# A fused attention and mixture-of-experts kernel: third group's operands stacked ahead of two weight quarters, twelve early scores, early first expert weights

## The reference, cut to what matters

```python
x = x + cross_attention(layernorm(x), ctx, ctx, k_length)     # x, ctx: (8, 256, 512)
x = x + moe(layernorm(x), gate_w, w1, b1, w2, b2, wd, wu, sw1, sb1, sw2, sb2, swd, swu)

# cross_attention: 8 heads of 32 rows per batch; out = softmax(s * q^T k) v, s = SCALE * log(k_length)
# moe, over T = 2048 tokens of D = 512:
probs = softmax(xt @ gate_w); top_p, top_i = top_k(probs, 2)       # 8 experts
for k in range(2):                                                 # capacity 320 per choice and expert
    h = gelu(buf @ w1 + b1); y = h @ w2 + b2 + gelu(buf @ wd) @ wu
    out += y[slot of the token] * keep * top_p[:, k]
sh = gelu(xt @ sw1 + sb1) @ sw2 + sb2 + gelu(xt @ swd) @ swu       # shared expert, for all tokens
out += 0.2 * sh
```

## Time and profile before

| | |
|---|---|
| median of 3 runs | 1408.8 us (1408.75 to 1411.6) |
| the profiled execution | 1401.34 us, span 1399.5 us |
| PE busy | 1346.4 us, 96% of the span |
| DVE busy | 812.6 us, 58% |
| ACT busy | 687.5 us, 49% |
| POOL busy | 249.1 us, 18% |
| mean granted clock of PE | 0.992 |

### The profile page before, as it was taken

The page is one execution under the profiler, slowest core; times in us unless marked ns, Lnnn a source line. Parts: engine busy times, 40 slices in busy tenths (PEclk is TensorE's granted clock), DMA queues, the critical chain, the costliest instruction groups (busy, mean ns, idle before and its releaser), DMA issues.

```text
span 1399.5 us, 27035 instructions
## 1 busy us (share of the span) xinstructions
PE 1346.4 (96%) x11193; PEld 967.1 (69%) x11211; DVE 812.6 (58%) x1313; ACT 687.5 (49%) x1023; POOL 249.1 (18%) x219
## 2 busy tenths in 40 slices
PE   5788999999999999999999999999999999999997
PEld 2152737364645555384788889998888888888895
DVE  7776778686978777762743625536255362452620
ACT  5866666667575756561523524335243342432511
POOL 4720010000000000452201304013030030300202
PEclk9999999999999999999999999999999999999999
DMA  9613131413131222118735665466454565553402
GB/s 273 203 37 100 52 93 39 113 39 106 46 96 49 84 54 92 24 25 213 233 102 124 168 131 157 126 149 164 130 157 109 134 178 131 151 132 99 99 6 38
DMA packets 136731, 155.89 MB, mean 111 GB/s; under 512 B 59049, under 2 KB 79673, under 8 KB 136610
## 3 DMA queue, kind: packets, MB, share of 16 engines
q1 hardware_dynamic: 124322, 128.97, 31.7%
q0 software_dynamic: 12288, 25.21, 9.6%
HBM read 109.47 MB, written 34.15 MB: 103 GB/s over the span
## 4 chain that ended last, share of the span: by engine, by line
PE 81%; DVE 8%; ACT 5%; issue 2%; DMA 1%; SPq 1%; POOL 1%; POOLq 0%; ACTq 0%; DVEq 0%
PE banks L1722 25%; PE banks L1752 24%; PE banks L1641 9%; PE banks L1659 6%; PE banks L1581 4%; PE banks L1561 3%; PE banks L1529 3%; DVE rowmax L1192 2%; DVE late_stage L1213 2%; ACT hidden L982 2%; PE banks L1774 1%; ACT QS L969 1%; PE banks L1615 1%; PE banks L1590 1%; SPq L801 1%
## 5 line engine op out<-in xcount | busy, mean ns | idle before, releaser
L1752 PE MATMUL banks<-hidden,w2h 128*128 128x0 bf16 x2048 | 313.0, 273 | 0.0
L982 ACT ACTIVATE hidden<-banks,scales 128x512 f32<-128x512 f32 x256 | 170.1, 686 | 111.8 <-PE banks L1561 92.4
L1752 PEld LDWEIGHTS banks<-hidden,w2h 128*128 128x128 bf16 x2048 | 198.4, 98 | 25.7
L1752 PE MATMUL banks<-hidden,w2l 128*128 128x0 bf16 x1024 | 195.7, 273 | 0.0
L1192 DVE TENSOR_REDUCE rowmax<-banks 128x1 f32<-128x512 f32 x256 | 172.7, 684 | 37.3 <-PE banks L1529 35.4
L1343 DVE TENSOR_TENSOR w1l<-stage,w1h 128x2048 bf16<-128x2048 f32 x32 | 73.4, 2292 | 199.7 <-ACT w1h L1058 199.7
L1075 ACT ACTIVATE hf<-banks,b1cols 128x640 f32<-128x640 f32 x128 | 101.7, 794 | 178.0 <-PE banks L1722 172.3
L1659 PE MATMUL banks<-w2h,hidden 128*128 128x512 bf16 x512 | 185.4, 381 | 0.0
L1082 ACT ACTIVATE yT<-banks 128x640 f32<-128x640 f32 (+1 forms) x32 | 22.1, 691 | 270.1 <-PE banks L1752 270.1
L1722 PE MATMUL banks<-eth,w1h 128*128 128x0 bf16 x1024 | 136.2, 276 | 3.2 <-ACT lowf L1065 3.2
L1722 PE MATMUL banks<-etl,w1h 128*128 128x0 bf16 x1024 | 136.8, 277 | 0.0
(11 more groups left out here) (194 smaller groups left out, 1963.3 us busy)
## 6 DMA issues: line engine op xcount, KB each, us to landing
stage<-in_L_ffn_w SPq DMA_DIRECT2D x64, 1024.0 KB, 5.5
split_parts<-hidden SPq DMA_DIRECT2D x16, 512.0 KB, 2.9
QS<-split_parts SPq DMA_DIRECT2D x48, 128.0 KB, 3.1
KS<-split_parts SPq DMA_DIRECT2D x48, 128.0 KB, 3.4
xin<-in_x SPq DMA_DIRECT2D x16, 256.0 KB, 3.6
cin<-in_ctx SPq DMA_DIRECT2D x16, 256.0 KB, 3.1
out_rows<-xin SPq DMA_DIRECT2D x16, 256.0 KB, 2.0
normed_rows<-x2r SPq DMA_DIRECT2D x16, 256.0 KB, 2.8
```

What stands on the lines that cost most here:

```text
L982: ac.activation(prob[n % NPH], bank(score_bank[unit]), ACT.Exp, scale=scales[:, g // 2:g // 2 + 1]).then_inc(s_exp, 1)
L1752: issued = mm(half_of(bank(b0 + j)).shape_from_register(bank_cols(e, j)), w[:, fb, rows], half_of(a[:, fb, :], j).shape_from_register(slot ...
```

## The change

- Quarters 6 and 7 are loaded in the first window, after the third group's `bounce` instead of before it. Quarters 2 to 6 are split in the exponentials' loops, and quarter 7 behind the first `up` block. The waits for the places that quarters 4 to 7 overwrite are counted per quarter.
- `EARLY_FIRST = 12` scores of the third group, instead of 8, run beside the second group's exponentials, from the third exponential on; the up pass of the first window has four fewer.
- `parts` and `rows` of the second group come in the last three units of the first group's loop; `b2_parts` comes at the first exponential of the second group instead of the tenth.
- `route` makes 14 (part 0) and 6 (part 1) empty steps ahead of `place`, instead of one each.
- The first three eighths of expert 0 are loaded at the seventh unit of the last window's up pass, into parts of `hidden` and into `late_stage`. `turn_x` of expert 0 waits until two of them are split. Splits 0 to 2 stand among the last downs, split 3 behind `e_rank` and `wu`.

```diff
+EARLY_FIRST = 12
...
-        yield
+
+        for _ in range(6 if part else 14):
+            yield
         add("place", part)
...
-                    score = scores((g + 1) * UNITS, (g + 1) * UNITS + EARLY)
+                    score = scores((g + 1) * UNITS, (g + 1) * UNITS + (EARLY if w else EARLY_FIRST))
...
-                if i >= (UNITS - EARLY if k else 2 if w else 1):
+                if i >= (UNITS - EARLY if k and w else 2 if k or w else 1):
                     next(score, None)
                     if k == 0 and w == 0 and i < 5:
                         next(score, None)
-                if k == 0 and w:
-                    if i == LATE + 2:
+                if k == 0:
+                    if i == (LATE + 2 if w else UNITS - 3):
                         add("parts", g + 1)
-                    elif i > LATE + 3:
+                    elif i > (LATE + 3 if w else UNITS - 3):
                         next(rows, None)
...
+                    if k == 0 and i == 7:
+
+                        add("w_load", 6)
+                        add("w_load", 7)
                     if k == 0 and i == 13:
                         add("wd", E)
-                    if k == 1 and i == 9:
+                    if k == 1 and i == 0:
                         add("b2_parts")
...
-            for _ in scores((a + 2) * UNITS + EARLY, (a + 3) * UNITS):
+            for _ in scores((a + 2) * UNITS + (EARLY if w else EARLY_FIRST), (a + 3) * UNITS):
...
+            if not more and n == 6:
+                add("first_stages")
...
             if w == 0:
+                if n == 1:
+                    split_quarter(7)
...
-    QUARTERS = (4, 8, 13, 18, 23, 28)
+    QUARTERS = (4, 8, 13, 18, 25)
...
-    for k in range(4, 8):
+    for k in range(4, 6):
         add("w_load", k)
...
     def first_weights():
         add("wd", 0)
-        for q in range(4):
+        for c in range(CH):
+            add("turn_x", 0, c)
+        for q in range(NST):
             for _ in range(6):
                 yield
             add("e_split", q)
-            if q == 0:
-                for c in range(CH):
-                    add("turn_x", 0, c)
...
         add("wu", e)
+        if e == 0:
+            add("e_split", NST)
...
+        first_stages = [hidden[:, 2 * FB * PASS + 2 * NPH * L:][:, 0:4096].bitcast(F32), late_stage[:, :],
+                        hidden[:, 2 * FB * PASS + NPH * L:][:, 0:4096].bitcast(F32)]
...
+                    if e == 0 and c == 0:
+
+                        sp.wait_ge(s_whi, split_no(1))
+                        sp.wait_ge(s_wlo, 2)
...
+                    n = j + NST - 1
+                    if j and n < 8 * E:
+                        sp.wait_ge(s_whi, split_no(n - NST))
+                        sp.wait_ge(s_wlo, n - NST + 1)
+                        load_quarter(n)
+                elif kind == "first_stages":
+
+                    sp.wait_ge(s_ones, len(SUMMED))
+                    sp.wait_ge(s_pv, GROUPS * QT)
+                    for n in range(NST):
+                        load_quarter(n)
...
+                    if n >= 4:
+
+                        pool.wait_ge(s_wlog, 12 if n < 6 else 16)
...
-                    if n == 4:
-                        act.wait_ge(s_wlog, 16)
+                    if n in (4, 6):
+
+                        act.wait_ge(s_wlog, 4 if n == 4 else 8)
```

More of the change, by code:

```diff
@@ L235, in exponentials_and_down @@
                     add("ones", g - 1)
-            if k == 0 and w == 0:
-                add("parts", 1)
             for _ in rows if k == 0 else ():
@@ L628, in build @@
                 w = g // 2
-                first = w == 0 or (unit[0] == "score" and g == 2 and i < EARLY)
+                first = w == 0 or (unit[0] == "score" and g == 2 and i < EARLY_FIRST)
                 if unit[0] == "score" and i < EARLY and g % 2 == 0 and g > 2:
@@ L682, in low_no, with stage_of @@
             return PASSES + e + 1
+        def stage_of(j):
+            return first_stages[j] if j < NST else stage[j % NST][:, :]
         def split_no(j):
@@ L690, in sync_program, with load_quarter @@
             dma = nc.sync.dma_start
+            def load_quarter(n):
+                e, q = divmod(n, 8)
+                src = (w1[e].rearrange("(k p) f -> p k f", p=P)[:, :, q * 512:q * 512 + 512] if q < 4
+                       else w2[e].rearrange("(k p) d -> p k d", p=P)[:, (q - 4) * 4:(q - 4) * 4 + 4, :])
+                dma(stage_of(n).rearrange("p (a w) -> p a w", w=512), src).then_inc(s_stage[n % NST], 16)
             for unit in plan:
@@ L803, in sync_program @@
                     j = unit[1]
-                    for n in range(3) if j == 0 else range(j + 2, j + 3):
-                        if n >= 64:
-                            continue
-                        if n >= NST:
-                            sp.wait_ge(s_whi, split_no(n - NST))
-                            sp.wait_ge(s_wlo, n - NST + 1)
-                        e, q = divmod(n, 8)
-                        src = (w1[e].rearrange("(k p) f -> p k f", p=P)[:, :, q * 512:q * 512 + 512] if q < 4
-                               else w2[e].rearrange("(k p) d -> p k d", p=P)[:, (q - 4) * 4:(q - 4) * 4 + 4, :])
-                        dma(stage[n % NST][:, :].rearrange("p (a w) -> p a w", w=512), src).then_inc(s_stage[n % NST], 16)
+                    n = j + NST - 1
[8 more added lines that the diff above has]
+                        load_quarter(n)
             n = GROUPS + (E - 1) * CH
@@ L1057, in act_program @@
                         dst = w2h[:, (q - 4) * 4:(q - 4) * 4 + 4, :]
-                    ac.activation(dst, stage[j % NST][:, :].rearrange("p (a w) -> p a w", w=512), ACT.Copy).then_inc(s_whi, 1)
+                    ac.activation(dst, stage_of(j).rearrange("p (a w) -> p a w", w=512), ACT.Copy).then_inc(s_whi, 1)
                 elif kind == "e_rank":
@@ L1342, in dve_program @@
                               else (w2l[:, (q - 4) * 4:(q - 4) * 4 + 4, :], w2h[:, (q - 4) * 4:(q - 4) * 4 + 4, :]))
-                    dv.tensor_tensor(lo, stage[j % NST][:, :].rearrange("p (a w) -> p a w", w=512), hi, ALU.subtract).then_inc(s_wlo, 1)
+                    dv.tensor_tensor(lo, stage_of(j).rearrange("p (a w) -> p a w", w=512), hi, ALU.subtract).then_inc(s_wlo, 1)
                 elif kind in ("route", "slot"):
@@ L1459, in shared_bank @@
                     pe.wait_ge(s_exp, 2 * UNITS)
-                    pe.wait_ge(s_max, 2 * UNITS + EARLY)
+                    pe.wait_ge(s_max, 2 * UNITS + EARLY_FIRST)
                 else:
```

## The result

The changed kernel took **1421.89 us** (median of 4 runs, 1420.91 to 1423.84), the kernel before 1408.78 (4 runs, three of them those of the table above; 1408.46 to 1411.6): by the comparison of the runs 1.0081 times as long, 95% interval 1.0059 to 1.0103, which is 8 to 15 us. By the medians it is 13.1 us slower, where 13 us less were forecast. The profiled execution took 1423.84 us, span 1422.0.

What follows compares the result with a forecast made beforehand. PE, busy for nearly the whole span, was taken to bound the kernel. Savings of 7.5 (opening with up pass) + 2.0 (first `place`) + 1.4 (second) + 2.1 (hand-over) = 13.0 us, off the 1408.8 median, gave 1395.8 us, range 1390 to 1403.

Steps and rivals of the forecast that it cites:

- The opening: First window up to and including its up pass: 6.5 us net before the pass plus 1.0 in it, bounds 2 and 11.3.
- Both signs that I had named for being wrong: PE waits for row maxima growing above 5 us in all; first up pass not shorter.
- Removed: 1.6 + 1.9 + 2.75 + 2.9 = 9.2 us: Opening: ACT's wait for POOL, quarter 7's copy, PE's row-maximum wait and the half clock all go; 2.7 us added back.
- The half clock, its largest term: Opening, 70 to 80 us: 5.8 us at the half clock disappear, saving 2.9 us of lost work.
- 1.5 us back for four maxima fewer: First up pass: of 2.1 us that PE waits for row maxima outside the long wait, 1.5 are saved.
- 0.5 us off for quarter 7's low pieces: First up pass: 4.50 us of POOL work moved there slows DVE, costing 0.5 us; net of the pass 1.0.
- First `place`: PE's 2.94 us wait and 1.8 us of clock go, 2.7 us return behind DVE's sum: 2.0 us, bounds 0.2 and 4.7.
- the stalls come back: Rival: waits before the eleventh exponential and third `e_up` each bring 1.8 us of half clock: 1398.9 us, chance 0.15.
- 3 × 1.3 us later: First `place`: POOL's scatters start that much later, covered by the gap before the second part's entries, at no cost.
- Second `place`: Placing two `up` blocks later finds DVE's counts ready, so PE's wait goes: 1.4 us saved.
- Hand-over: Into expert 0: 4.9 us go, 0.3 and 1.9 (third `e_up`) return; 2.1 us taken, bounds −1 and 4.9.
- the landing of the second load: Hand-over: loads for splits 3 and 4, issued near 658.4, land at 663.7 and 666.4; PE then waits 1.9 us.

Runs made afterwards that it cites:

- fourth set: On a slower chip (kernel before 1413.91 us), changed kernel with two loads ahead of the transposes, plus: quarter 7's split moved back, 1415.09; `parts` and `rows` back, 1414.23; both, 1416.26.
- faster kind: The two chips on which the unchanged kernel before took 1400.2 and 1399.8 us; the changed kernel took 1404.42 us on one of them.
- slower kind: The two chips on which the unchanged kernel before took 1412.7, 1413.9 and 1413.9 us in three sets.
- first set: On a slower chip (kernel before 1412.73 us): changed kernel again, 1422.55; with early loads moved back, 1427.13; with both delays undone, 1416.06; kernel before plus hand-over alone, 1412.99.
- the spaced variant: Changed kernel with scatters from the sixth group on held to one per two up blocks, the rest in a burst later: 1411.35 us, 1.0072 times the kernel before.

## Why the prediction was wrong

**The opening (forecast 7.5, measured a loss).** Its parts came much as written: the stacking copies of the third group at 43.23, `b2_parts` in one block (from 53.29, not near 50), no half clock in 70 to 80 us. That the 3.58 us of issuing mean a full ring is a reading that no run tests. But the first `rank` came at 76.44, 1.5 us earlier and not 7, and the up pass took 24.8 us from its first to its last block instead of 22.1. Both signs that I had named for being wrong are there, 5.3 us of waits for row maxima and a pass that isn't shorter. The step that failed is the sum "Removed: 1.6 + 1.9 + 2.75 + 2.9 = 9.2 us": it adds up stalls of engines that wait for one another as if each lay on the path. The idle times in it went, and others took their place. The half clock, its largest term, moved and did not shrink:

```profile
50.00:60.00 10.00, 8.15 (x37) 1.58 (x29) 6.19 (x9) 6.92 (x10) 3.63 (x4) 0.70 0.71 233
90.00:100.00 10.00, 6.95 (x87) 5.47 (x83) 8.31 (x20) 5.72 (x15) 1.58 (x2) 0.83 0.08 28
```

Before, these two stretches had 0.83 and 1.00; over 44 to 104 us the mean granted clock is 0.91 in both kernels, and TensorE is busy 46.7 us before and 46.6 after. At the start, TensorE's timeline after:

```profile
48.60 0.41 PE L1576 MATMUL banks<-identb,MS 128*32 128x128 bf16 x16 [1.91 <-DVE MS L1234]
48.83 1.60 PE L1614 MATMUL banks<-hidden,ones_f 128*32 128x512 f32 x8
50.20 1.93 PE L1614 MATMUL banks<-hidden,VT 128*32 128x512 f32 x8
52.07 0.61 PE L1594 MATMUL banks<-QS,KS 128*128 128x512 bf16 x1
54.11 0.38 PE L1594 MATMUL banks<-QS,KS 128*128 128x512 bf16 x1 [1.43 <-issue]
```

The value products run at the half clock and stand before group 0's last exponential; ScalarE idles 3.65 us for it, and the second group's first exponential comes at 54.1 instead of 51.8 us. Yet the order of before did not mend that (fourth set), so this reading of the cause fell.

For the up pass I had taken 1.5 us back for four maxima fewer: between 76 and 103 us the waits for row maxima grew from 2.2 to 3.4 us. And I had taken 0.5 us off for quarter 7's low pieces, from the time of a subtraction set against that of a cast, two different operations. The kernel after has the same four operations with GpSimd idle:

```profile
54.89 0.68 DVE L1221 TENSOR_TENSOR b2parts<-b2f,b2parts 9x512 bf16<-9x512 f32 x1
```

They take 0.41, 0.68, 0.41 and 0.68 us there, against 0.77, 1.53, 1.26 and 1.52 beside GpSimd's pieces before. So `b2_parts` fell from 5.1 to 2.2 us by its move, and VectorE is held up by more than I took. GpSimd and VectorE in the up pass, timelines after:

```profile
88.25 2.78 POOL L908 TENSOR_TENSOR w2l<-late_stage,w2h 128x512 bf16<-128x512 f32 x2
```

```profile
88.97 1.04 DVE L1274 TENSOR_TENSOR xin<-xin,rden 128x512 f32<-128x512 f32 x1
89.94 1.24 DVE L1352 TENSOR_TENSOR hidden<-hf,hidden 128x128 bf16<-128x128 f32 x1
91.10 0.68 DVE L1225 TENSOR_REDUCE rowmax<-banks 128x1 f32<-128x512 f32 x1
```

The two operations take 0.68 and 0.28 us in the kernel before; 1.3 us are lost, TensorE waits 1.66 us for the maximum behind them and then runs some 3.5 us at the half clock (0.69 and 0.88 granted in the two stretches of 4 us from 92). The term was 3.7 us wrong (1.0 us gain forecast, 2.7 lost). With the quarter's split moved back the two operations take 0.68 and 0.28 us again and the pass loses 0.5 us only. How the 2.2 us split between the maximum's wait and the clock is not shown: with `parts` moved back and the pieces still there, the operations and the wait are as long, but the clock stays at 1.00 and the pass loses 1.2; with both moved back the long wait is gone, and the pass still loses 1.7. The Trainium skill ("SBUF — State Buffer", the section on SBUF's two separate sides) has a VectorE operation with two SBUF inputs and a GpSimd operation that reads SBUF exclude each other on their shared ports, for the whole instruction. That allows up to the 2.78 us of these pieces; the 1.3 us measured lie between nothing and that. Why the opening's start never gained is not settled. Neither of its moved pieces alone, nor both, changed the end of the first pass by more than the traces of one opening differ (98.9 to 101.9 us with that of before, 101.1 to 103.1 with the changed one).

**First `place` (forecast 2.0).** The wait went, and came back behind DVE's sum, as forecast, but with the half clock too. ScalarE after, where before it waited 0.99:

```profile
580.77 1.27 ACT L1014 ACTIVATE hidden<-banks,scales 128x512 f32<-128x512 f32 x2 [3.36 <-DVE late_stage L1246]
```

TensorE waits 2.46 us behind it and then runs some 3.4 us at the half clock (0.71 and 0.87 granted in the two stretches of 4 us from 580). That is the rival "the stalls come back". The stage 112–122 takes 63.5 to 63.6 us in the four traces with the delay on the faster kind, and 62.1 to 65.2 in six on the slower; with the opening changed and the delay undone it takes 65.3. Beside the 62.2 or 63.9 of before, the 2.0 us of gain are not there, and a gain or loss by the delay itself is not told from the rest. The same edit cost more elsewhere, by the second step that failed, one that I had priced at nothing: "POOL's scatters start after the `rstd2` step [...] 3 × 1.3 us later [...] no cost". Three more scatters then stood in the row in front of TensorE's late increments: 122 to 128 take 24.6 to 24.9 us in all four traces on the slower kind with the first placing where it was, 28.8 to 29.2 in all six with it fourteen steps later. That is the 4.5 us of the table. Undoing both delays gave 6.5 us: in the traces 4.0 us lie here and 3.6 in the hand-over, less 1.7 for the second `place`.

**Second `place` (forecast 1.4).** Right: 1.4 to 1.7 us.

**Hand-over (forecast 2.1, measured −3.4 to −4.3).** The wait at the third `e_up` was named at the right place and as the right mechanism: splits 3 and 4 stand before ScalarE's first expert Gelu. The third step that failed is its size, the landing of the second load. SP's queue and ScalarE after, to set beside the earlier trace rows:

```profile
664.94 1.34 SPq L829 DMA_TRANSPOSE eth<-xg  x1
...
680.44 1.07 SPq L713 DMA_DIRECT2D stage<-in_L_ffn_w  x2
```

```profile
691.30 1.91 ACT L1091 ACTIVATE w2h<-stage 128x2048 bf16<-128x2048 f32 x1 [3.62 <-DMA stage<-in_L_ffn_w]
```

```profile
694.08 1.98 PE L1755 MATMUL banks<-eth,w1h 128*128 128x0 bf16 x8 [5.70 <-ACT hf L1108]
695.86 1.99 PE L1755 MATMUL banks<-etl,w1h 128*128 128x0 bf16 x8
```

I had the second load land 8.0 us after 658.4 (5.3 for the first, 2.7 more); ScalarE starts on it 10.9 us after the two were issued, and the half clock followed. The wait is 5.7 instead of 1.9 us.

The wait is not the hand-over edit's alone. With the hand-over by itself, and with both delays undone (first set), the two loads stand behind the transposes as well, yet TensorE waits only 0.1 us at the third `e_up`, and 144–149 takes 50.3 and 51.1 us (50.75 in the kernel before). In these two TensorE ends the last downs 3.3 and 4.8 us later, counted from the end of block 128: the wait at the second `place` is still there, and another of 2.7 us in the downs. SP issues `wuf` only then: 4.5 and 7.3 us after the second load, where the kernel after has 0.5. In the first of them ScalarE starts on that load 8.3 us after its issue without having idled; in the kernel after on the faster kind it lands 10.1 us after its issue. So the loss needs TensorE early and the late loads together. Whether `wuf`'s transfers stretch the second load is not tested.

On the faster kind, two loads moved ahead in the same queue turned this stage from +3.4 to −4.1 us, and are what makes the difference between a slower and a faster kernel.

**The reference time.** I subtracted a saving worked out in a 1401.34 us execution from a median of 1408.8. The 7.4 us between them were in view: the traced execution was below the lowest of the runs, so it was not one of their kind. By the later traces of the kernel before on the slower kind, what they had, and it lacked, was a stall that one edit could lengthen; the timed runs of the result themselves left no trace that would show it.

## What to carry to other kernels

When the profiled execution is faster than every timed run, look for what it doesn't show before summing anything against it. Set stages against each other by several traces: one trace of the kernel before differed from the next by 1.7 us in one stage. Idle times of engines that feed each other are one loss, not several; where a stall goes, the next one must be priced with the clock it brings. In a queue that issues in order, what is wanted first goes first: two loads ahead of ten transposes were worth 8.1 us here.

## What the runs showed of the hardware

Beside a row of GpSimd's indirect scatters (one each 1.28 us, 15 to 18 of them) TensorE's semaphore increments rose up to 18 us late on one kind of chip, and the granted clock fell to 0.50 (1.2 GHz) meanwhile; on the other kind the same programs have them 0.02 us after the product. It is shown that the scatters bring it (14.2 us less without them, on the slower kind) and that the length of the row counts (15 against 18 in it: 4.2 us). The increments that ScalarE and VectorE made in the same stretch came on time, as far as they are on record. What holds TensorE's back, and why only on some chips, is open. The Trainium skill ("VectorE: DVE Perf Modes", the section on the TRN2 errata) warns that increments at a high rate from one engine can deadlock another, and advises to space them; no run here can show whether that is the same thing, since the spaced variant ran on a chip without the stall.

Beside GpSimd's subtractions VectorE's operations take longer: the four operations of `b2_parts` take 5.1 us together in all nine traces in which such pieces run beside them, and 2.2 us in all eleven in which GpSimd is idle.
